# State-space loop with turn and output one place sooner and token turns late; the last module's gate in eight units there instead of in the attention

## What is computed

```
decay = exp(-exp(w)) * (0.5 + 0.5 * tf)           # per feature and batch
ek = exp(min(k, 30));  ekv = ek * v               # k = v = fside
nf, df = forward scans of ekv, ek;  nb, db = reverse scans
num = nf + nb - ekv + exp(min(u + k, 30)) * v
den = df + db - ek  + exp(min(u + k, 30))
gate = sigmoid(x) * num / max(den, 1e-8) * (0.8 + 0.2 * tf)

x = x + attention(gate(x, w0, u0))                # 16 heads
x = x + ternary_ffn(gate(x, w1, u1))
x = x + state_space(gate(x, w2, u2))              # 64 heads, chunks of 32 tokens
x = x + experts(gate(x, w3, u3))                  # 8 experts, top 2
```

## Time and profile before

| | us |
|---|---|
| median of 3 runs | 716.97 |
| the runs | 722.58, 716.97, 716.85 |
| the profiled execution, its own time | 719.14 |
| its span, first to last instruction | 717.3 |

### The profile page before, as it was taken

The page is one execution under the profiler, slowest core; times in us unless marked ns, Lnnn a source line. Parts: engine busy times, 40 slices in busy tenths (PEclk is TensorE's granted clock), DMA queues, the critical chain, the costliest instruction groups (busy, mean ns, idle before and its releaser), DMA issues.

```text
span 717.3 us, 13912 instructions
## 1 busy us (share of the span) xinstructions
PE 557.5 (78%) x5668; PEld 403.4 (56%) x5668; DVE 405.2 (56%) x597; ACT 370.4 (52%) x791; POOL 147.3 (21%) x115
## 2 busy tenths in 40 slices
PE   0187868577967686668999999998639999999980
PEld 0044546454545571345564556666528999997560
DVE  5889998868899367883755545453461121111223
ACT  6986887457786615754557555644321222222212
POOL 1000000000000125841009555520010322322210
PEclk9995687785597999988999999998758999999996
DMA  9500000000000100000000000000049999889825
GB/s 354 163 1 1 1 1 1 1 0 1 1 1 1 30 1 1 0 1 1 1 3 2 2 3 2 3 2 2 31 164 383 422 419 379 307 329 339 309 124 190
DMA packets 18479, 71.38 MB, mean 100 GB/s; under 512 B 4848, under 2 KB 9968, under 8 KB 14704
## 3 DMA queue, kind: packets, MB, share of 16 engines
q1 hardware_dynamic: 15408, 64.20, 23.6%
q0 software_dynamic: 1920, 5.25, 2.0%
q10 hardware_dynamic: 1088, 1.05, 0.4%
HBM read 65.77 MB, written 4.72 MB: 98 GB/s over the span
## 4 chain that ended last, share of the span: by engine, by line
PE 56%; DVE 26%; ACT 10%; issue 4%; DMA 2%; POOL 1%; SPq 0%; ACTq 0%; DVEq 0%; POOLq 0%
PE PS L1416 41%; DVE nmx L1017 3%; DVE arena L930 3%; DVE arena L927 3%; PE PS L1891 2%; PE PS L1454 2%; PE PS L1960 2%; ACT arena L604 1%; PE PS L1667 1%; DVE A L949 1%; PE PS L1532 1%; ACT arena L764 1%; DVE arena L1121 1%; PE PS L1492 1%; DMA arena<-ypair 1%
## 5 line engine op out<-in xcount | busy, mean ns | idle before, releaser
L1416 PE MATMUL PS<-arena 128*128 128x128 f32 (+6 forms) x1376 | 162.1, 296 | 17.1 <-DVE arena L1121 10.1
L1416 PEld LDWEIGHTS PS<-arena 128*128 128x128 f32 (+4 forms) x1376 | 129.3, 167 | 43.0 <-issue 26.1
L604 ACT ACTIVATE arena<-PS,nmx 128x128 f32<-128x128 f32 (+1 forms) x128 | 52.1, 424 | 44.8 <-DVE nmx L1017 44.8
L1469 PE MATMUL PS<-ident,arena 128*128 128x128 f32 x192 | 37.6, 350 | 32.6 <-ACT arena L591 30.5
L1364 DVE TENSOR_TENSOR R<-arena,PS 128x128 f32<-128x128 f32 x16 | 4.6, 288 | 89.3 <-ACT arena L858 89.2
L1469 PEld LDWEIGHTS PS<-ident,arena 128*128 128x128 f32 x192 | 29.1, 181 | 40.4 <-ACT arena L604 25.7
L383 POOL TENSOR_SCALAR arena<-ident,gcol 128x128 f32<-128x128 f32 x4 | 2.4, 601 | 234.0 <-DMA gcol<-in_gcol 234.0
L443 POOL TENSOR_TENSOR arena<-arena 128x1024 f32<-128x1024 f32 x16 | 37.8, 2367 | 41.1 <-DVE arena L1203 33.1
L475 POOL DMA_INDIRECT ypair<-arena,oid x20 | 19.8, 988 | 122.5 <-ACT arena L864 122.5
L1416 PE MATMUL PS<-arena,R 128*128 128x256 f32 x192 | 44.2, 380 | 0.6 <-ACT arena L864 0.6
L1416 PEld LDWEIGHTS PS<-arena,R 128*128 128x128 f32 x192 | 35.2, 190 | 5.1 <-issue 1.0
(11 more groups left out here) (299 smaller groups left out, 1202.9 us busy)
## 6 DMA issues: line engine op xcount, KB each, us to landing
arena<-in_moe SPq DMA_DIRECT2D x23, 1408.0 KB, 6.6
arena<-in_moe SPq DMA_DIRECT2D x23, 768.0 KB
inproj<-in_inproj SPq DMA_DIRECT2D x1, 1344.0 KB, 10.5
arena<-in_fT SPq DMA_DIRECT2D x1, 1024.0 KB, 4.9
xT<-in_xT SPq DMA_DIRECT2D x1, 1024.0 KB, 5.4
R<-in_w1T SPq DMA_DIRECT2D x1, 1024.0 KB, 7.4
R<-in_w2T SPq DMA_DIRECT2D x1, 1024.0 KB, 9.4
R<-in_w3T SPq DMA_DIRECT2D x1, 1024.0 KB, 11.5
```

Source lines behind the costliest of these rows:

```text
L604: sc.activation(pr[u % 2][:, j, 0:n], PS[:, 2 * (u % 2) + j // 2, (j % 2) * 256:(j % 2) * 256 + n], ACT.Exp, bias=nmx[:, u % 2, j:j + 1], ...
L1416: last = mm(dst, l, r, start=(n == 0), stop=(n == len(pairs) - 1))
L1469: last = nc.tensor.transpose(PSB[:, 4 * HALF + c:4 * HALF + c + P], pr[u % 2][:, j, k * P:(k + 1) * P], ident[:])
```

## The change

Six things change.

1. Only gates 1 to 5 stay in the attention (`GATES = 6`), and they are spread thinner, `FRAME = 7`: five gates of seven places are again 35. The pair of scans of a `gate_step` 1 or 2 is split: 1 and 2 are now the forward scan alone, 7 and 8 the correction and the reverse scan.
2. The factor of the last module (gates 6 and 7) is made in eight units of 256 columns in the state-space loop, unit `i` beside tile `i`. A unit reads its slice of `fT` again from memory (one transfer of 128 KB per unit on SP's queue), uses the stretches `uf`, `uek` and so on, and is one `unit_min`, `unit_den`, `unit_num` and `unit_out` on VectorE and one `unit_inputs` and `unit_guess` on ScalarE. Its decay is a broadcast column, not a written row.
3. TensorE: `turn(i-1)` moves ahead of `state(i,2)`, `output(i-1)` ahead of `segments(i+1,2)`, the first two segments ahead of `state(i,1)`, and `tokens(i+1)` back to just before `within(i)`.
4. `tokens(i+1)` now waits for `add_out(i-1)` and `turned(i-1)`, where it waited for `add_out(i-2)` and `turned(i-2)`.
5. VectorE: the loop reads `gated(i-1)`, `unit_out(i-1)`, `unit_den(i)`, `unit_num(i)`, `unit_min(i+1)`, `add_out(i-1)`, `front(i+1)`. So `add_out` comes one tile sooner and behind the unit.
6. ScalarE: `turned` and `inverse_root` follow that order, with `unit_guess(i)` ahead of `inverse_root(i-1)` and `unit_inputs(i+1)` behind `by_chunk(i+1)`.

The core of the diff:

```diff
@@ sync
-            sp.wait_ge(S["dve_R"], 8)
-            sp.wait_ge(S["act_euk"], 16)
+            sp.wait_ge(S["dve_R"], 6)
+            sp.wait_ge(S["act_euk"], 12)
...
+            sp.wait_ge(S["dve_num"], GATES)
+            for t in range(UNITS):
+                c, ct, n, cols = unit_of(t)
+                if t:
+                    sp.wait_ge(S["act_euk"], 2 * GATES + 3 * t)
+                load(uf[t % 2], a["fT"][:, c, cols], "f")
@@ scalar
+            def unit_inputs(t):
+                c, ct, n, cols = unit_of(t)
+                act.wait_ge(S["dve_fmin"], CT + t + 1)
+                if t:
+                    act.wait_ge(S["dve_num"], GATES + t)
+                done(sc.activation(uek, uek, ACT.Exp))
+                sc.activation(uxe, uek, ACT.Copy, scale=dq[:, 3, ct, n:n + 1]).then_inc(S["act_euk"], 1)
+                sc.activation(ufc, uf[t % 2], ACT.Copy, scale=cb[:, n:n + 1]).then_inc(S["act_euk"], 1)
+                sc.activation(ug, uf[t % 2], ACT.Exp, bias=wu[:, 3, 1, ct:ct + 1]).then_inc(S["act_euk"], 1)
+
+            def unit_guess(t):
+                act.wait_ge(S["dve_den"], GATES + NCH + t + 1)
+                done(sc.activation(udb, udf, ACT.Relu, bias=tiny[:, 0:1]))
+                done(sc.activation(udb, udb, ACT.Ln, bias=tiny[:, 1:2]))
+                sc.activation(udb, udb, ACT.Exp, scale=-1.0).then_inc(S["act_guess"], 1)
@@ vector
                 if k in (1, 2):
                     dve.wait_ge(S["act_decay"], 4 * (i + 1))
                     dve.wait_ge(S[name], 4 * (i + 1))
                     done(v.tensor_tensor_scan(y, dmat[:, 0:N], x, 0.0, ALU.mult, ALU.add))
+                if k in (7, 8):
                     ends = y.rearrange("p (a b t) -> p a b t", a=CT, b=2)[:, :, :, T - 1]
...
             def gate_part(n):
                 i, k = 1 + n // FRAME, n % FRAME
-                for part in ((0,), (2,), (3,), (5, 6), ())[k]:
+                for part in ((0,), (2,), (8,), (3,), (5, 6), (), ())[k]:
                     gate_step(i, part)
-                if n == 3:
+                if n == 4:
                     gate(0, 1)
-                if k == 4 and i < 7:
-                    gate_step(i + 1, 1)
+                if k >= 5 and i < GATES - 1:
+                    gate_step(i + 1, 1 if k == 5 else 7)
...
+            def unit_scan(t, x, y):
+                c, ct, n, cols = unit_of(t)
+                d = dec[:, 3, ct, n:n + 1].broadcast_to([P, T])
+                done(v.tensor_tensor_scan(y, d, x, 0.0, ALU.mult, ALU.add))
+                done(v.tensor_tensor(y[:, T - 1:T], y[:, T - 1:T], rdq[:, 3, ct, n:n + 1], ALU.mult))
+                done(v.tensor_tensor_scan(y[:, 0:T - 1][:, ::-1], d[:, 1:T], y[:, 0:T - 1][:, ::-1], y[:, T - 1:T], ALU.mult, ALU.add))
...
             for i in range(NT):
                 if i:
                     gated(i - 1)
-                if i >= 2:
-                    add_out(i - 2)
+                    unit_out(i - 1)
+                unit_den(i)
+                unit_num(i)
+                if i + 1 < NT:
+                    unit_min(i + 1)
+                if i:
+                    add_out(i - 1)
                 if i + 1 < NT:
                     front(i + 1)
@@ tensor
             def tokens(i):
-                if 1 <= i <= 2:
-                    pe.wait_ge(S["dve_xw"], i)
-                    pe.wait_ge(S["dve_tok"], i)
-                if i >= 3:
-                    pe.wait_ge(S["act_hgt"], i - 2)
-                    pe.wait_ge(S["dve_x"], X_FFN + i - 2)
+                if i == 1:
+                    pe.wait_ge(S["dve_xw"], 1)
+                    pe.wait_ge(S["dve_tok"], 1)
+                if i >= 2:
+                    pe.wait_ge(S["act_hgt"], i - 1)
+                    pe.wait_ge(S["dve_x"], X_FFN + i - 1)
...
             for i in range(NT):
-                state(i, 1)
                 if i + 1 < NT:
                     segments(i + 1, 0)
                     segments(i + 1, 1)
-                    tokens(i + 1)
+                state(i, 1)
+                if i:
+                    turn(i - 1)
                 state(i, 2)
                 state(i, 3)
+                if i:
+                    output(i - 1)
                 if i + 1 < NT:
                     segments(i + 1, 2)
                     segments(i + 1, 3)
                 if i % 2 == 0:
                     state(i, 4)
+                if i + 1 < NT:
+                    tokens(i + 1)
                 within(i)
-                if i:
-                    turn(i - 1)
                 between(i)
-                if i:
-                    output(i - 1)
@@ constants
-FRAME = 5
+FRAME = 7
+GATES = 6
+UNITS = 8
```

76 lines of the change are left out of this document (56 added, 20 removed).

## The result

| | us |
|---|---|
| before, median of 4 runs | 716.9 (716.2 to 722.6) |
| after, median of 4 runs | 730.6 (728.4 to 730.9) |
| after / before | 1.0166, 95% interval [1.0120, 1.0213] |
| profiled execution of after | 730.56, span 728.8, mean granted clock 0.862 |

The change is slower by 1.7%. The time lies in the range on record, and the forecast's likeliest case, no change within 1%, is not what came.

What follows compares the result with a forecast made beforehand. VectorE was taken to bound the attention, TensorE at full clock the state-space loop. 26 us gained and 29 lost make +3 on the profiled 719.1, so 722, or 720 against the median; range 702 to 736 us.

Steps and rivals of the forecast that it cites:

- likeliest case: Whole kernel: no change within 1%, at 720 us, given 38%; alone it spans 711 to 727.
- The attention: Attention: gates taken off VectorE gain 12 us in the first half, 6 between, 8 in the second; 26 in all.
- Rival 3: Attention: TensorE at 1.2 GHz bounds all wide steps, so 12 us gained in place of 26; 734 us, 15%.
- The units' own times: State-space loop, VectorE: a unit's scans take 0.69 and 0.75 us, a pass 0.42; with gaps 6.95 us per tile.
- The lock: State-space loop: VectorE stands still during GpSimd's instructions, 2.8 us in odd periods and 4.0 in even ones.
- Head and end: State-space loop: `front(1)` comes 8.2 us later at the head; 4.5 us come back at the end.
- The clock term: State-space loop: TensorE's low clock after its waits adds 3 us over the loop, bounds 0 and 14.
- The chain's 22: State-space loop, tile 1 to 7: VectorE's serial chain of 15.3 us plus GpSimd blocking gives 110 us for 88.1, 22 lost.
- Rival 2: State-space loop: TensorE's clock falls in every tile while it waits for `tokens` or `turn`, 14 us lost for 3; 731 us, 20%.
- the signs named ahead: State-space loop: forecast, periods about 19 us, TensorE waiting for `add_out`; second rival, clock well under 0.9, TensorE ending last.

Runs made afterwards that it cites:

- attention_only: The changed kernel's attention with six gates, the state-space loop in the order of the kernel before, no units anywhere; 693.6 us, ratio 0.964 to before.
- no_units: The changed kernel with every instruction of the eight units left out, loads included, new loop order kept; 711.8 us, ratio 0.986 to before.
- warm2: The changed kernel with four dummy matrix products on TensorE at each of two places where it waited in the loop; 725.4 us, ratio 1.009 to before.
- small_pool: The changed kernel with GpSimd's three instructions per tile in the state-space loop cut to one head; 704.4 us, ratio 0.974 to before.
- order_only: The kernel before with only the new order of the state-space loop on TensorE, ScalarE and VectorE, no units; 737.6 us, ratio 1.022 to before.

## Why the prediction was right and wrong

**The attention: right in sum.** Forecast 26 us, in the profiled execution 23.3, by attention_only 25.5 (uncertain by 2.5). By part 12, 6 and 8 were forecast; first half 14.1 and middle 6.3. The second half is 0.8 here and 4.1 to 4.3 in attention_only, no_units and warm2 (66.1 to 66.3 us from its first to its last maxima, 69.5 in after), with the same instructions: some 3 us of it are this execution's own (no_units is 2.5 longer in the first half instead). Another 2.8 us come behind the last maxima, where I had put nothing, and the first maxima start 0.75 later. Rival 3 falls.

**The units' own times: right** to 0.02 us each, but for `unit_min` (0.29 for 0.42 at most). The lock was there too, and smaller than reckoned: each blocked instruction ended 0.3 to 0.4 us after GpSimd's, and VectorE lost 1.9 us in a long period and 3.6 in a short one for the 2.8 and 4.0 that I had reckoned. The Trainium skill's rule (page "SBUF — State Buffer", section "SBUF: two separate sides"), that VectorE with two SBUF inputs and GpSimd lock each other out for a whole instruction, agrees with this: small_pool cuts the GpSimd work and the lengths return to 0.56 and 0.43. The short periods (18.2, 18.2, 18.8, where the forecast had 15.3 + 4.0) are VectorE's chain as worked out: `add_out` waits for nothing there. Two slips in the working change little: the mean of 2.8 and 4.0 is 3.4 and not 3.5 (0.6 us over six periods), and slice 9 of VectorE's row has 6 tenths, not 8 or 9.

**Head and end: the size right, the cause half.** +8.2 and -3.9 for +8.2 and -4.5. But of the head's 8.2 order_only has 4.7 with no unit in it.

**The clock term: the term that was sized wrong.** The loop's stretch lost 30.5 us. The chain's 22 leaves 8.5 of them for the term "I take 3 us over the loop; bounds 0 and 14", and all of it lies in the three long periods. By the forecast's terms (15.3, with 4.0 of lock in a short period and 2.8 in a long one, 2.7 less in the last) the short ones were to take 57.9 us and took 55.2; the long ones were to take 51.6 and took 63.4. In warm2, with the clock held up, the two longest of them are 5.7 us shorter in sum. What was wrong in the working is the sentence that "`add_out` stands behind `unit_num` and comes later still". In the long periods it waited 2.43, 2.65 and 1.06 us for the inverse root. I had priced `tokens` at 1.2 GHz, and had `output` and the segments only "nearly" on the chain in odd periods; what ran at 1.2 GHz was the turn, the states and the sums (7.0 us for 3.9), which the new order puts ahead of `tokens`. Rival 2 named this place, its condition (stretched by more than 0.7 us) and its time, 731, though beside the turn it priced the output and the segments, which ran at or near full clock, and not the states and the sums. It got 20%, on the ground that the clock was 1.00 throughout the loop of before. That was a row of an order in which TensorE hardly waited (85.3 of 88.1 us busy). Of the signs named ahead, those of the forecast came in the short periods (18.2 us, TensorE waiting for `add_out`) and those of rival 2 in the two longest, where TensorE ended last at a clock of 0.77 and 0.78.

**Whose loss it is: missed.** The prediction gave the loop's loss to the units. By the runs the order alone has 15.5 us and the units 22, and neither is a property of its own: on the old order the same units cost 55. By the prediction's own chain, without the unit's 7 us, order_only's stretch would have stayed at TensorE's 88; it took 108. On the profiled executions the forecast was 722 and the measured time 730.6: 2.7 of the 8.5 us between them lie in the attention and 5.8 in the loop. That the loop's total came this near is in part luck, since the reason given is half the true one, and the time lies in the range because the range reached into rival 2.

## What to carry to other kernels

Where one engine is busy all the time at full clock, a wait put in front of it can be paid twice: as the wait, and in what it runs slowly afterwards (2.7 and 4.2 us in order_only's long periods). So place added work by the waits that already stand in the time line of each engine that it touches, ScalarE's too, rather than by the idle sum of one; the parts of four units in such waits cost 1.5 us, the same parts elsewhere 10. And when a change both moves an order and adds work, run the order alone first.
